# The fourth pair's norm moved into layer 1's turns, and VectorE's norm work of a turn moved behind the finish

## The reference

```
xn = layernorm(x)
s  = L0_attn(xn)      # a decaying complex recurrence along the sequence
f  = L0_ffn(xn)       # 32 experts, top 4 of each token, plus a shared expert
x  = x + s * silu(f)
xn = layernorm(x)
s  = L1_attn(xn)      # softmax attention inside each sequence
f  = L1_ffn(xn)       # 8 experts of width 64, top 2, gelu
return x + s * silu(f)
```

## Time and profile before

| what | us |
|---|---|
| median of 3 runs (456.02 to 461.48) | 456.53 |
| the profiled execution's own time | 457.9 |
| its span, first to last instruction | 456.0 |
| PE busy / PEld busy | 381.0 / 349.4 |
| VectorE busy | 319.6 |
| ScalarE busy | 257.6 |
| POOL busy | 275.7 |
| mean granted PE clock | 0.94 |

### The profile page before, as it was taken

One profiled execution on the slowest core, in us unless ns is written; L12 is line 12 of the kernel. 1 busy time (PEld: TensorE's weight loads), 2 busy tenths in 40 slices (PEclk: granted clock), 3 DMA queues, 4 the chain that ended last, 5 costly groups with the idle time before them and its releaser, 6 DMA issues. The chain is left out here.

```text
span 456.0 us, 8825 instructions
## 1 busy us (share of the span) xinstructions
PE 381.0 (84%) x2582; PEld 349.4 (77%) x2582; DVE 319.6 (70%) x1153; ACT 257.6 (56%) x505; POOL 275.7 (60%) x324
## 2 busy tenths in 40 slices
PE   0596986995089999997999897967998998889994
PEld 0584875884089999996999797856987977779983
DVE  6869588769137667766567648682699999995643
ACT  2233124421046767764776564537898886788882
POOL 5935777777777777763777777527777877100000
PEclk9999798898579999999999998978999999899998
DMA  7899995111257667537677563412222222000000
GB/s 183 257 376 310 291 390 180 53 54 46 90 176 213 215 224 219 201 127 240 196 227 217 171 207 101 139 54 56 64 60 70 67 58 65 24 14 25 12 24 23
DMA packets 45902, 65.16 MB, mean 143 GB/s; under 512 B 8586, under 2 KB 23331, under 8 KB 45859
## 3 DMA queue, kind: packets, MB, share of 16 engines
q1 hardware_dynamic: 37666, 47.83, 33.0%
q0 software_dynamic: 8192, 16.79, 12.6%
HBM read 28.93 MB, written 35.65 MB: 142 GB/s over the span
## 5 line engine op out<-in xcount | busy, mean ns | idle before, releaser
L550 POOL DMA_INDIRECT slot_rows<-xn_tok,slot_of x128 | 126.8, 991 | 49.7 <-issue 38.7
L564 POOL DMA_INDIRECT onehot<-expert_rows,slot_of x64 | 64.9, 1014 | 38.3 <-DMA expert_rows<-zeros 19.4
L564 POOL DMA_INDIRECT route_tmp<-expert_rows,slot_of x64 | 63.0, 985 | 19.5 <-issue 19.5
L1399 DVE TENSOR_TENSOR act<-sg,ps 128x384 f32<-128x384 f32 x48 | 26.5, 553 | 49.5 <-ACT sg L1007 48.6
L738 PE MATMUL ps<-w_dn,actT 96*128 x384 | 53.1, 283 | 5.1 <-ACT zeros L1016 5.1
L738 PEld LDWEIGHTS ps<-w_dn,actT 96*128 96x128 f32 x384 | 48.1, 197 | 5.9 <-issue 5.9
L1007 ACT ACTIVATE sg<-ps 128x384 f32<-128x384 f32 x48 | 23.5, 489 | 37.9 <-PE ps L747 37.2
L722 PE MATMUL ps<-ident,rows 128*128 128x128 f32 x192 | 29.9, 280 | 13.2 <-DMA rows<-slot_rows 11.6
L747 PE MATMUL ps<-w_gu,raw_fc 128*128 x192 | 37.8, 342 | 1.2 <-DVE act L1399 0.5
L1016 ACT COPY zeros<-ps 128x512 f32<-128x512 f32 x48 | 28.1, 585 | 17.7 <-PE ps L738 17.6
L824 PE MATMUL ps<-prT,rows 128*128 128x128 f32 x256 | 34.4, 291 | 3.4 <-DVE raw_fc L1548 3.4
(11 more groups left out here) (240 smaller groups left out, 899.1 us busy)
## 6 DMA issues: line engine op xcount, KB each, us to landing
slot_rows<-zeros SPq DMA_DIRECT2D x12, 1024.0 KB, 12.0
rows<-slot_rows SPq DMA_DIRECT2D x48, 256.0 KB
expert_rows<-zeros SPq DMA_DIRECT2D x48, 256.0 KB
x_tok<-in_L_attn_x_dram SPq DMA_DIRECT2D x8, 256.0 KB, 5.5
slot_rows<-xn_tok,slot_of POOLq DMA_INDIRECT x128, 2.4
out_dram<-raw_fc SPq DMA_DIRECT2D x16, 128.0 KB, 1.8
w_dn<-in_L_ffn_w_down_dram SPq DMA_DIRECT2D x1, 1536.0 KB, 17.1
onehot<-expert_rows,slot_of POOLq DMA_INDIRECT x64
```

The lines of the kernel that those rows point to most:

```text
L550: g.indirect_dma_start(out=slot_rows[r], out_offset=bass.IndirectOffsetOnAxis(ap=slot_of[:, n:n + 1], axis=0), in_=xn_tok[:, r * HT + t, : ...
L564: g.indirect_dma_start(out=gath[b % 4][:, j, :], out_offset=None, in_=expert_rows[r], in_offset=bass.IndirectOffsetOnAxis(ap=slot_of[:, n: ...
L1399: v.tensor_tensor(act[u][:].rearrange("p (a b) i -> p a b i", a=2), sg[u][:].rearrange("p (a b) i -> p a b i", a=2), ps[:, 1 + 2 * u:3 + 2 ...
```

## The change

1. `NORM_AT` gives pair 3 turn 2 of layer 1, and not the end of layer 0 (key -1). `sum_experts(7)` goes to turn 1, its `tanh_f` and `mix` too, statistics and `norm1` to turn 2, `turn_xn` and `copy_xn` to turn 3, logits to turn 4. `sum_experts(6)` stays in layer 0. `silu_f(3)` is gone from ScalarE's last stages. `BATCHES` has one batch more: pairs 2 and 3 each have their own.
2. Layer 1's first products (`project(0)`, `values(0)` on PE, their copies on ScalarE) stand inside the last stage of layer 0, `down` of the last stage writes bank 0 and so does not wait for the copy before it, and `hidden_of(0)` stands ahead of the wait for the last copy.
3. In every turn, VectorE's `stats1`/`rstd1` or `sum_experts` stand behind `finish` and the gates, not ahead of the reciprocal.
4. The first pass of `finish` signals by a semaphore of its own, `d_moe_read`; `expert_sum` and `tanh_moe`, which overwrite what that pass reads, wait for it and not for `d_fin`.

```diff
-NORM_AT = {-1: 3, 4: 4, 6: 5, 8: 6, 10: 7}
-BATCHES = ((0, 2), (2, 2), (4, 1), (5, 1), (6, 1), (7, 1))
+NORM_AT = {2: 3, 4: 4, 6: 5, 8: 6, 10: 7}
+BATCHES = ((0, 2), (2, 1), (3, 1), (4, 1), (5, 1), (6, 1), (7, 1))
...
-        if b >= 0 and turned(b + ahead) is not None:
+        if b > 0 and turned(b + ahead) is not None:
...
+        def down_bank(n):
+            return 0 if n == N - 1 else 6
...
-                if not first:
+                if not first and n < N - 1:
                     pe.wait_ge(e_out, n)
...
+            def first_products():
+                pe.wait_ge(biases, 2)
+                pe.wait_ge(c_lgs, FSEQ // 2 - 1)
+                pe.wait_ge(e_act, N - 1)
+                project(0)
+                values(0)
...
-                    pe.wait_ge(d_fin, b)
+                    pe.wait_ge(d_moe_read, b)
...
-            project(0)
-            values(0)
+            pe.wait_ge(e_out, N - 1)
             scores(0)
+            pe.wait_ge(e_act, N)
+            hidden_of(0)
+            pe.wait_ge(e_out, N)
...
-                if step == 2:
+                if step == 2 and q < FSEQ // 2 - 1:
                     after = lambda: silu_f(q)
+                if n == N - 1:
+                    turn = first_kept
...
-            rstd1()
-            norm1(FSEQ // 2 - 1)
...
                 dve.wait_ge(d_mth, b + 1)
-                link(v.scalar_tensor_tensor(out=mg[:].rearrange("p a d -> p (a d)"), in0=mth[:], scalar=1.0,
-                                            in1=bank(3, SEQ), op0=ALU.add, op1=ALU.mult))
+                if b:
+                    dve.wait_ge(d_fin, b)
+                v.scalar_tensor_tensor(out=mg[:].rearrange("p a d -> p (a d)"), in0=mth[:], scalar=1.0,
+                                       in1=bank(3, SEQ), op0=ALU.add, op1=ALU.mult).then_inc(d_moe_read, 1)
+                dve.wait_ge(d_moe_read, b + 1)
...
                 u = b % 2
-                if turned(b) is not None:
-                    stats1(turned(b))
-                    rstd1(summed(b))
-                elif summed(b) is not None:
-                    sum_experts(summed(b))
                 dve.wait_ge(d_p, b + 1)
...
                 if turned(b) is not None:
+                    stats1(turned(b))
+                    rstd1(summed(b))
                     norm1(turned(b))
+                elif summed(b) is not None:
+                    sum_experts(summed(b))
                 if turned(b + 1) is not None:
                     mix(turned(b + 1), True)
```

More of the change, by code:

```diff
@@ L96, in gated @@
 def gated(b):
-    if b == -1:
-        return 0
-    for k, (first, count) in enumerate(BATCHES[1:], 1):
+    if b in (-1, 0):
+        return b + 1
+    for k, (first, count) in enumerate(BATCHES[2:], 2):
         if turned(b - 2) == first + count - 1:
@@ L365, in build @@
         d_fin = sem("d_fin")
+        d_moe_read = sem("d_moe_read")
         stored = [sem(f"stored{u}") for u in range(2)]
@@ L734, in down @@
                 pe.wait_ge(e_aTs, n + 1)
-                if not first:
+                if not first and n < N - 1:
                     pe.wait_ge(e_out, n)
                 for j in range(GT):
-                    mm = pe.matmul(ps[:, 6, j * P:(j + 1) * P], actT[u][:, j * P:(j + 1) * P],
+                    mm = pe.matmul(ps[:, down_bank(n), j * P:(j + 1) * P], actT[u][:, j * P:(j + 1) * P],
                                    w_dn[:, bass.ds(e[j] * P, P)], start=True, stop=True)
@@ L797, in stage_e, with turned_rows, project, values @@
                     down(n, n % 2, ids(n * GT))
+            def turned_rows(b):
+                return xn_tok[:, b * 2:b * 2 + 2, :]
+            def project(b):
+                pe.wait_ge(c_xn_kept, b // 2 + 1)
+                if b:
+                    pe.wait_ge(d_nmx, b)
+                pe.matmul(ps[:, 6 if b else 1, 0:SEQ], w1T[:, 0:P], turned_rows(b), start=True, stop=True).then_inc(d_qk, 1)
+            def values(b):
+                if b:
+                    pe.wait_ge(d_vs, b)
+                for j in range(2):
+                    pe.matmul(ps[:, 7, j * VW:(j + 1) * VW], ones_bf[:], bv_rows[:], start=True, stop=False)
+                    mm = pe.matmul(ps[:, 7, j * VW:(j + 1) * VW], turned_rows(b)[:, j, :], w1T[:, P:P + VW],
+                                   start=False, stop=True)
+                mm.then_inc(d_v, 1)
             for n in range(N):
@@ L807, in _ @@
                     turn = lambda: logits_between(q - 1)
+                if n == N - 1:
+                    turn = first_products
                 if half_starts(n):
@@ L810, in _ @@
                 stage_e(n, turn)
-            pe.wait_ge(e_out, N)
-            pe.wait_ge(c_lgs, FSEQ // 2 - 1)
             def expert_sum(b, u, first):
@@ L840, in _ @@
             pe.wait_ge(biases, 2)
[L842 to L860, removed]
             def scores(b):
@@ L900, in output @@
                 mm.then_inc(d_o, 1)
-            project(0)
-            values(0)
+            pe.wait_ge(e_out, N - 1)
             scores(0)
+            pe.wait_ge(e_act, N)
+            hidden_of(0)
+            pe.wait_ge(e_out, N)
             for b in range(NSEQ):
                 u = b % 2
-                hidden_of(b)
+                if b:
+                    hidden_of(b)
                 if b:
@@ L1015, in copy_out @@
                     sc.wait_ge(e_stored[slot], rnd * 16)
-                a.copy(eo[slot], bank(6)).then_inc(e_out, 1)
+                a.copy(eo[slot], bank(down_bank(n))).then_inc(e_out, 1)
             for r in range(NH):
@@ L1065, in stage_e, with shift_projected, keep_values, first_kept @@
                     after()
+            def shift_projected(b):
+                sc.wait_ge(d_qk, b + 1)
+                if b:
+                    sc.wait_ge(d_s, b)
+                a.activation(key_of, ps[:, 6 if b else 1, 0:SEQ], ACT.Identity, bias=w1T[:, 2 * P + 1:2 * P + 2],
+                             scale=-SCALE).then_inc(d_qks, 1)
+            def keep_values(b, u):
+                sc.wait_ge(d_v, b + 1)
+                if b >= 2:
+                    sc.wait_ge(d_o, b - 1)
+                a.copy(v_sb[u], ps[:, 7, 0:2 * VW].rearrange("p (a d) -> p a d", a=2)).then_inc(d_vs, 1)
+            def first_kept():
+                sc.wait_ge(biases, 2)
+                shift_projected(0)
+                keep_values(0, 0)
             def tanh_gates(k):
@@ L1085, in _ @@
                     after = lambda: tanh_gates(0)
+                if n == N - 1:
+                    turn = first_kept
+                    sc.wait_ge(sent[1], 16 * HT * TOP0)
                 if half_starts(n):
@@ L1088, in _ @@
                 stage_e(n, turn, after)
-            sc.wait_ge(sent[1], 16 * HT * TOP0)
             def tanh_f(p):
@@ L1099, in tanh_moe @@
                 if not first:
-                    sc.wait_ge(d_fin, b)
+                    sc.wait_ge(d_moe_read, b)
                 a.activation(mth[:], bank(3, SEQ), ACT.Tanh, scale=0.5).then_inc(d_mth, 1)
@@ L1114, in _ @@
             sc.wait_ge(biases, 2)
[L1116 to L1131, removed]
             for b in range(NSEQ):
@@ L1521, in _ @@
                     sum_experts(2 * q)
[L1522 to L1527, removed]
-                    rstd1()
+                if q < FSEQ // 2 - 1:
+                    if step == 2:
+                        sum_experts(2 * q + 1)
+                    if step == 3:
+                        mix(q, False)
+                        stats1(q)
+                    if step == 4:
+                        rstd1()
                 if n == SG - 1:
@@ L1532, in _ @@
                     hidden(n + 1, (n + 1) % 2)
-                if step == 2 and n == N - 2:
-                    sum_experts(2 * q + 1)
-            rstd1()
-            norm1(FSEQ // 2 - 1)
             def finish(b, u, first, used):
                 dve.wait_ge(d_mth, b + 1)
-                link(v.scalar_tensor_tensor(out=mg[:].rearrange("p a d -> p (a d)"), in0=mth[:], scalar=1.0,
-                                            in1=bank(3, SEQ), op0=ALU.add, op1=ALU.mult))
+                if b:
+                    dve.wait_ge(d_fin, b)
+                v.scalar_tensor_tensor(out=mg[:].rearrange("p a d -> p (a d)"), in0=mth[:], scalar=1.0,
+                                       in1=bank(3, SEQ), op0=ALU.add, op1=ALU.mult).then_inc(d_moe_read, 1)
+                dve.wait_ge(d_moe_read, b + 1)
                 dve.wait_ge(d_os, b + 1)
```

## The result

The changed kernel takes **487.01 us** (median of 4 runs, 484.18 to 487.48) against 456.89 for the kernel before (4 runs, 456.02 to 461.48): a ratio of 1.063, 95% interval 1.056 to 1.070. The forecast was 480.4, range 468 to 488. The profiled execution took 487.01, its span 485.2 (before 456.0), VectorE's busy time 321.0 (before 319.6). So VectorE does nearly the same work, in 29 us more.

The account below looks back on a forecast made before the run. VectorE was taken as the bound in layer 1 from turn 2 to turn 10. Turn 11 24.8 us later and -0.9 at the end made +23.9: 481.8 for the profiled execution, 480.4 us median, range 468 to 488.

Parts of the forecast that it names:

- a border that gains only 2.9 us: Border of the layers: lower bound of the gain, 2.9 and not 8.5 us, adding 5.6 to the range's upper end.
- 2.4 for the clock: Layer 1: PE's spread (0.61 us) doubled at half clock in four pairs, +2.4 us, also added to the range's upper end.
- Part 1: Border of the layers: PE runs on without waiting, `least(0)` starts near 298.5, `gate_hidden(1)` at 314.6, 8.5 us gained.
- Part 2: Turns 1 and 2 of layer 1: pair 3 adds 8.1 us of VectorE work that before lay on the border's path.
- Part 3: Turns of layer 1: `tanh_f` waits for VectorE's late sum, holding ScalarE once per pair; a pair takes 25.9 us, before 20.14.
- 8.0 us from the sum's end to `gate_hidden`: Odd into even turns: ScalarE's stretch from `tanh_f` to the spread's end, 8.0 us, with VectorE standing still 5.8.
- the rival at 483: Layer 1: PE falls to half clock after ScalarE's halt, only the spread on the path, +2.4 us; chance 0.20.
- Part 4: `expert_sum` and `tanh_moe` start up to two passes earlier: -0.9 us in the last turn; nothing was the other bound.
- up to turn 10 PE does not bound, so nothing: Layer 1 up to turn 10: the early signal gains nothing, since PE was not taken as the bound there.
- ScalarE isn't held: Odd turns: VectorE reaches the sum before ScalarE reaches `tanh_f`, so the wait is free; 453.5 us, chance 0.08.
- only the round trip counts: Odd turns: VectorE waits 0.7 us ahead of `mix` five times, ScalarE's next turn otherwise covered; 457 us, chance 0.07.
- The drain: ScalarE's table switches: about 1380 ns each by the page, 13.8 us for ten loads on the path; left out of the sum.

Follow-up runs that it names:

- run 2: The kernel before with only VectorE's statistics and sums moved behind `finish` and the gates; 482.43 us, ratio 1.050 to before.
- run 8: The kernel before with only the early signal of `finish`'s first pass added; 456.75 us against 460.02, ratio 0.994.
- run 1: The changed kernel with VectorE's statistics, `rstd1` and sums back at the turn's start; 457.28 us against 458.69 before, ratio 0.997.
- run 3: The changed kernel with the odd turns' sums back at the turn's start, even turns' statistics still late; 456.89 us, ratio 0.997 to before.
- run 4: The changed kernel with the even turns' statistics and `rstd1` back at the turn's start, odd turns' sums still late; 475.89 us, ratio 1.036 to before.
- run 5: The changed kernel with ScalarE's `tanh_f` moved behind the next turn's gelu, VectorE's order untouched; 465.79 us, ratio 1.015 to before.
- run 6: The changed kernel with 72 extra PE products ahead of the logits in all five turns with logits; 488.28 us, ratio 1.061 to before.
- run 7: The changed kernel with 72 extra PE products ahead of the logits in turns 4, 6, 8 and 10 alone; 482.16 us, ratio 1.052 to before.

## Why the prediction was right, and which terms were off

The direction, the mechanism and its place were as forecast; the time lay 6.6 us above it, 1.0 inside the range. That it lay inside is in part luck: the upper end, 488, is 480.4 with 5.6 for a border that gains only 2.9 us and 2.4 for the clock. The rows don't give the 2.9 (with the old pace and the old step to turn 1 they leave 8.5 - 3.3 - 1.8 = 3.4); the border gained 6.2, and the clock cost more than its 2.4, 3.1 us in three pairs (80.76 for 3 x 25.9). The table has 5.3 of the 6.6; the other 1.3 is the step from the profiled execution to the median, 1.4 before and nothing after, where the profiled execution is the median. Step by step, for `gate_hidden`:

| turn | forecast | measured | later by |
|---|---|---|---|
| 1 | 314.6 | 317.23 | 2.6 |
| 2 | 328.2 | 330.92 | 2.7 |
| 4 | 350.7 | 353.50 | 2.8 |
| 6 | 376.6 | 380.26 | 3.7 |
| 8 | 402.5 | 407.26 | 4.8 |
| 10 | 428.4 | 434.26 | 5.9 |
| 11 | 437.9 | 443.70 | 5.8 |
| span | 479.9 | 485.2 | 5.3 |

- **Part 1, the border: steps right, anchor off.** From the last `act_T` to `least(0)` the forecast's rows gave 298.5 - 293.74 = 4.8; it took 300.42 - 295.81 = 4.6. From `least(0)` to exp 2.3 (300.42 to 302.69), as forecast, with the table load on the path; exp to `gate_hidden(0)` 5.81 for 5.84. To `gate_hidden(1)` it took 8.73, and 8.0 was taken: turn 1 waits 2.54 for gelu. The rest, 2.1, is where layer 0 ended: the last `act_T` started at 293.74 in the execution shown of before, but at 296.67 and 296.54 in runs 2 and 8, whose layer 0 has the same code (rows above), and in the other profiled executions between 294.31 and 297.44. The forecast hung on the earliest one. Over the kernels measured, `gate_hidden(1)` stands at 322.8 to 325.1 with the old border (before, runs 2 and 8) and at 315.7 to 318.7 with the new one and pair 3 behind it (the change and runs 1, 3 to 7), on the mean 6.2 us earlier: inside the bounds, below the 8.5.
- **Part 2** was right that pair 3's work eats this: with early order (run 1) turn 2 follows turn 1 after 330.88 - 318.62 = 12.3 us, before after 7.65, and the kernel ends where before does.
- **Part 3, the hold at `tanh_f`: right in kind, mis-sized.** Runs 1, 2 and 5 show it from three sides. The term "8.0 us from the sum's end to `gate_hidden`" measured 9.2 (398.06 to 407.26), and VectorE's standstill 6.9 for 5.8. The sum priced PE's part at the old trace's clock. That was the rival at 483, which saw the halt of 5 us (4.63) but put the wrong row on the path: the spread, which it doubled, takes 0.60 as before, and what the low level stretches is `expert_sum`, `turn_gates` and `values`, which stand ahead of the spread on PE and now end after ScalarE's gates. With PE kept busy the 8.0 us are 7.95 and a pair takes 25.7, the forecast 25.9, and run 7, at 482.2 and a ratio of 1.052, comes to the forecast's 5.2% (1.5 us of which it owes to the last `expert_sum`). So forecast and rival held together: the hold as priced, and the clock on top of it, at 1.1 us a pair from turn 4 to turn 10 and not 0.6.
- **Part 4: the term right, a reason wrong.** The -0.9 at the end is there: 1.70 us (475.85 to 477.55) from the last `gate_hidden` to `expert_sum`, before 2.61. But "up to turn 10 PE does not bound, so nothing" does not hold for the kernel before: turns 5, 9 and 11 together gain 2.2 us from the signal (run 8), and the earlier trace rows had one of these waits. In the change the hold covers them; only turn 12 gained 0.5, and from turn 11 to the end it took 41.5 us for 42.85.
- The cases that ScalarE isn't held and that only the round trip counts fell: VectorE waits for spread and exp in every even turn. Exp starts 0.02 us behind the table load's end (302.67), and the loads cost their 1.28 alone. The drain that the Trainium skill's page "ScalarE: Activation LUTs" (What ACT_TABLE_LOAD costs) adds to each switch, and that the forecast left out, does not show here.

Not settled: the last `expert_sum` takes 3.46 to 3.77 us in the profiled executions of some kernels (before, the change, runs 2, 5 and 6), at a granted clock of 0.50 to 0.55, and 2.04 in the others, at 1.00. That is worth 1.4 us in a comparison of single executions, of run 8 with before too, and what decides which level the clock has there was not tried.

## What to carry to other kernels

When an instruction is moved later on one engine, look at who waits for it and what stands behind that waiter in its own in-order queue: here 2 us of sums, moved by half a turn, held ScalarE's whole next turn, and 27 us stood where 20 had. Look also for work that can fill the engine's wait for the answer: the statistics, left between `mix` and the reciprocal, would have covered two fifths of the loss (run 4). The new halt of PE, 4.63 us, had to be priced with everything that PE ran behind it at the low level up to the next hand-over (`expert_sum` alone 3.76 for 2.03), and not with the last instruction only.

## What had not been expected

- Two moves that cost nothing (statistics late) and 3.6% (sums late) cost 6.3% together; their costs don't add.
- Extra products on PE gave 3.5 us back in three pairs where PE stood idle anyway, and cost 3.7 us in the one turn where it did not.
- A signal two short passes earlier was worth 0.6% on the kernel before, by removing small waits of VectorE for PE in turns 5, 9 and 11 (2.2 us by the rows; the first two lie in a stretch where VectorE was read as the bound) and by 0.9 us at the end.
